# Cross attention of a perceiver: text probabilities and value sums turned together with the image probabilities, one DMA back, queries made per batch

## What is computed

```python
def attend(q, k, v):                       # scale 64 ** -0.5
    attn = softmax(einsum('bihd,bjhd->bhij', q, k) * SCALE)
    return einsum('bhij,bjhd->bihd', attn, v)
out = attend(x @ Wq, txt @ Wk, txt @ Wv) + attend(x @ Wq, img @ Wk_ip, img @ Wv_ip)
x = x + out @ Wo + bo                      # text and image have a softmax each
```

## Time and profile before

| | |
|---|---|
| median of 3 runs | 2453.11 us (2441.91 to 2453.33) |
| the profiled execution | 2435.73 us |
| its span (first to last instruction) | 2433.6 us |
| PE busy, share of the span | 2160.2 us, 89% |
| DVE busy | 1570.4 us, 65% |
| ACT busy | 925.0 us, 38% |
| POOL busy | 877.5 us, 36% |
| mean granted TensorE clock | 0.94 of full speed |

### The profile page before, as it was taken

One profiled execution on the slowest core, in us unless ns is written; L12 is line 12 of the kernel. 1 busy time (PEld: TensorE's weight loads), 2 busy tenths in 40 slices (PEclk: granted clock), 3 DMA queues, 4 the chain that ended last, 5 costly groups with the idle time before them and its releaser, 6 DMA issues. The chain is left out here.

```text
span 2433.6 us, 37422 instructions
## 1 busy us (share of the span) xinstructions
PE 2160.2 (89%) x13637; PEld 1726.1 (71%) x13637; DVE 1570.4 (65%) x2756; ACT 925.0 (38%) x1869; POOL 877.5 (36%) x535
## 2 busy tenths in 40 slices
PE   5878877796699999999999999999999997787897
PEld 3445545464598889888898998998998994334684
DVE  4179934333577677677677677777776763795554
ACT  1166611210244344344344444444443443452331
POOL 1066412431343333243343333343333300362455
PEclk8989977798899999999999999999999998798898
DMA  5800002511476677677676777776776656001364
GB/s 159 169 16 14 8 1 88 230 50 57 145 200 184 185 218 205 185 217 206 185 217 180 226 202 208 198 207 199 202 211 186 194 156 248 4 0 44 98 148 114
DMA packets 229957, 362.99 MB, mean 149 GB/s; under 512 B 41920, under 2 KB 197824, under 8 KB 225168
## 3 DMA queue, kind: packets, MB, share of 16 engines
q1 hardware_dynamic: 223008, 342.08, 48.1%
q0 software_dynamic: 6768, 18.49, 3.2%
HBM read 234.97 MB, written 125.50 MB: 148 GB/s over the span
## 5 line engine op out<-in xcount | busy, mean ns | idle before, releaser
L2271 PE MATMUL img_ps<-cn,pt_hi 128*128 128x256 f32 (+1 forms) x3072 | 569.7, 287 | 3.0 <-DVE pt_lo L2478 3.0
L2271 PEld LDWEIGHTS img_ps<-cn,pt_hi 128*128 128x128 f32 (+1 forms) x3072 | 477.3, 191 | 3.2 <-issue 3.2
L2271 PE MATMUL img_ps<-cn,pt_lo 128*128 128x256 f32 (+1 forms) x1536 | 435.9, 284 | 0.0
L2466 DVE STREAM_TRANSPOSE prob_blocks<-prob 128x384 f32<-128x384 f32 x512 | 250.6, 547 | 183.8 <-ACT prob L2402 175.9
L2248 PE MATMUL s_ps<-ct,a_hi 128*128 128x508 f32 x768 | 315.7, 411 | 0.0
L2249 PE MATMUL s_ps<-ct,a_hi 128*128 128x508 f32 x768 | 304.2, 396 | 0.0
L2250 PE MATMUL s_ps<-ct,a_lo 128*128 128x508 f32 x768 | 304.0, 396 | 0.0
L2001 POOL TENSOR_SCALAR ct<-staged 128x762 fp32r<-128x762 f32 x64 | 136.8, 2138 | 439.6 <-DMA staged<-in_ctx_t 312.5
L2271 PEld LDWEIGHTS img_ps<-cn,pt_lo 128*128 128x128 f32 (+1 forms) x1536 | 292.6, 190 | 0.0
L2478 DVE TENSOR_TENSOR pt_lo<-prob_moved,pt_hi 128x768 fp32r<-128x768 f32 x256 | 277.9, 1124 | 9.4 <-ACT pt_hi L2414 9.2
L2001 POOL TENSOR_SCALAR cn<-staged 128x768 fp32r<-128x768 f32 x64 | 137.4, 2147 | 376.5 <-DMA staged<-in_ctx_n 293.4
(11 more groups left out here) (370 smaller groups left out, 3712.9 us busy)
## 6 DMA issues: line engine op xcount, KB each, us to landing
prob_rows<-prob_blocks SPq DMA_DIRECT2D x512, 192.0 KB, 2.1
prob_moved<-prob_rows SPq DMA_DIRECT2D x512, 192.0 KB, 3.6
staged<-in_ctx_n SPq DMA_DIRECT2D x64, 384.0 KB, 4.7
staged<-in_ctx_t SPq DMA_DIRECT2D x64, 381.0 KB, 4.7
up_all_m<-in_up SPq DMA_DIRECT2D x8, 2048.0 KB, 12.8
down_all_m<-in_down SPq DMA_DIRECT2D x8, 1024.0 KB, 23.4
sums_m<-y_b SPq DMA_DIRECT2D x63, 128.0 KB, 2.2
w_shared<-in_wq SPq DMA_DIRECT2D x7, 1024.0 KB, 7.3
```

Source lines behind the costliest of these rows:

```text
L2271: last = nc.tensor.matmul(img_ps[:, 0:D], left[0:n, j, :], rows[0:n, right, j, :], start=j == 0 and at == 0, stop=j == IB - 1 and at == 2)
L2466: nc.vector.transpose(blocks[:, m], source[:, m]).then_inc(turned, 1)
```

## The change

- **One bundle.** `prob` grows from 12 to 15 blocks of 128 columns: 12 of image probabilities, one of text probabilities, two of the sums. The four DVE transposes, the stores and the return carry all of them. Text (of step `g-2`) and sums (of step `g-2`) are put into `prob` by ACT and DVE in turn `g` and leave with bundle `g+1`. So `turn_text`, `turn_sums`, their PSUM banks and the copies `pt_txt` and `ot` go, and `value_side` runs one turn later and reads `moved` itself.
- **Stores and return.** Each of the four parts is stored as 32 rows of each of four row groups (`block_rows[s, m]`, read as `c a f`), so that the whole bundle comes back with one DMA, 7680 bytes to a partition. `moved` is one buffer, not two: the return of bundle `g` waits until `pt_lo` of step `g-1` is made (`split_done`), until `value_side(g-4)` is copied out (`valued`), and until all four parts are stored.
- **Sums.** `img_ps` is used over its full width: one matmul of 512 columns takes `pt_hi` with the high and the low part of `cn`, and one of 256 columns adds `pt_lo` with the high part into the second half. ACT scales the second half into `o_part`, DVE scales the first and adds `o_part` (SCALAR_TENSOR_TENSOR), into `prob`.
- **Text.** The exponentials of the text go to three buffers `txt_prob`; ACT, no longer DVE, multiplies them by the reciprocal.
- **Queries per batch.** `queries(b)` makes one batch (64 columns) in one bank, at the end of the 7th and the 14th turn of a tile, and ACT alone copies it. `wq` and `wo` are loaded in halves, `wq` after the returns of the 5th and 6th turn, `wo` after those of the 15th and 16th.
- `project` comes two turns later than before and stands behind `key_side`.

```diff
+    TXT_AT, O_AT = IB, IB + 1
+    BUNDLE = IB + 1 + C
+    RUN = BUNDLE * QR
+    LAG = 3
-        block_rows = nc.dram_tensor("prob_rows", (2, Q, P, RUN), F32).ap()
-        moved = [sb(f"prob_moved{s}", [P, Q, IB, QR]) for s in range(2)]
+        block_rows = nc.dram_tensor("prob_rows", (2, Q, QR, Q, RUN), F32).ap()
+        moved = sb("prob_moved", [P, Q, BUNDLE, QR])
...
+            return {6: 2 * i + 1, 13: 2 * i + 2 if i < NT - 1 else None}.get(n) if g < N else None
...
-            for g in range(N):
+            for g in range(N + LAG):
                 if g >= 2:
-                    sp.wait_ge(moved_in[s], 16 * Q * (g // 2))
+                    sp.wait_ge(moved_in, 16 * (g - 1))
                 for m in range(Q):
                     sp.wait_ge(turned, Q * g + m + 1)
-                    sp.dma_start(block_rows[s, m], blocks[:, m].rearrange("p j r -> p (j r)")).then_inc(stored[m], 16)
-                if g >= 2:
-                    sp.wait_ge(split_done, 2 * (g - 1))
+                    sp.dma_start(block_rows[s, m].rearrange("c a f -> a c f"),
+                                 blocks[:, m].rearrange("p j r -> p (j r)")).then_inc(stored[m], 16)
+                if g:
+                    sp.wait_ge(split_done, 2 * min(g, N))
+                if g > LAG:
+                    sp.wait_ge(valued, g - LAG)
                 for m in range(Q):
                     sp.wait_ge(stored[m], 16 * (g + 1))
-                    sp.dma_start(moved[s][m * QR:(m + 1) * QR].rearrange("c a j r -> c a (j r)"),
-                                 block_rows[s, m].rearrange("(a c) f -> c a f", a=Q)).then_inc(moved_in[s], 16)
+                sp.dma_start(moved[:].rearrange("p a j r -> p (a j r)"),
+                             block_rows[s].rearrange("m c a f -> (m c) (a f)")).then_inc(moved_in, 16)
...
-                        for at, (left, right) in enumerate(((pt_hi, 0), (pt_hi, 1), (pt_lo, 0))):
-                            last = nc.tensor.matmul(img_ps[:, 0:D], left[0:n, j, :], rows[0:n, right, j, :],
-                                                    start=j == 0 and at == 0, stop=j == IB - 1 and at == 2)
+                        nc.tensor.matmul(img_ps[:], pt_hi[0:n, j, :], rows[0:n, :, j, :], start=j == 0, stop=False)
+                        last = nc.tensor.matmul(img_ps[:, D:2 * D], pt_lo[0:n, j, :], rows[0:n, 0, j, :],
+                                                start=False, stop=j == IB - 1)
...
+                pe.wait_ge(moved_in, 16 * (g + LAG + 1))
...
-                        nc.tensor.matmul(out, wv[:, c, cols], ot[:, c, rows], start=c == 0, stop=False)
+                        nc.tensor.matmul(out, wv[:, c, cols], moved[:, rows, O_AT + c, :], start=c == 0, stop=False)
...
+                    nc.scalar.activation(o_part[:], img_ps[:, D:2 * D], ACT.Copy,
+                                         scale=inv[(g - 2) % 3][:, 1:2]).then_inc(part_kept, 1)
+                    act.wait_ge(turned, Q * min(g + 1, N + LAG))
+                    nc.scalar.activation(prob[:, TXT_AT * P:TXT_AT * P + TXT], txt_prob[(g - 2) % 3][:], ACT.Copy,
+                                         scale=inv[(g - 2) % 3][:, 0:1]).then_inc(txt_normed, 1)
...
+                    nc.vector.scalar_tensor_tensor(out=prob[:, O_AT * P:], in0=img_ps[:, 0:D],
+                                                   scalar=inv[(g - 2) % 3][:, 1:2], in1=o_part[:], op0=ALU.mult,
+                                                   op1=ALU.add).then_inc(sums_kept, 1)
```

More of the change, by code:

```diff
@@ L2209, in kept, with queries @@
                 pe.wait_ge(t_kept[place[0]], place[1])
[L2211 to L2221, removed]
+            def queries(b):
+                bank = use()
+                for p in range(PAIRS1):
+                    for c in range(C):
+                        last = nc.tensor.matmul(t_ps[bank][:, p * S:(p + 1) * S], wq[:, c, p * P:(p + 1) * P],
+                                                k.h_t[:, c, b * S:(b + 1) * S], start=c == 0, stop=c == C - 1)
+                last.then_inc(t_done[bank], 1)
+                return ring.place(1)
             def key_side(g):
@@ L2311, in _ @@
             pe.wait_ge(wq_in, 16)
[L2312 removed]
+            q_place = queries(0)
             pe.wait_ge(wk_in, 16)
[L2314 to L2315 removed]
+            kept(q_place)
             a_place = key_side(0)
[L2317 removed]
+            for g in range(N + LAG + 2):
                 if g < N:
@@ L2386, in keep_a, with keep_queries @@
                 nc.scalar.activation(flat(a_hi), t_ps[bank][:, 0:D], ACT.Copy).then_inc(a_hi_kept, 1)
+            def keep_queries(b):
+                bank, count = ring.next()
+                act.wait_ge(t_done[bank], count)
+                act.sem_inc(queried, 1)
+                for r in range(2):
+                    rows = slice(r * HD1, (r + 1) * HD1)
+                    last = copy(q[rows, :, b % 2, r, :], t_ps[bank][rows, :].rearrange("p (j n) -> p j n", j=PAIRS1))
+                last.then_inc(t_kept[bank], 1)
             act.wait_ge(q_zeroed, 1)
-            keep_queries(act, copy, 0, ring)
+            keep_queries(0)
             keep_a(0)
-            for g in range(N + 3):
-                if 1 <= g <= N:
-                    keep(act, copy, ring, pt_txt[(g - 1) % 3][0:TXT, :], TXT, P)
-                if g >= 3:
-                    keep(act, copy, ring, flat(ot), P, D)
-                if not boundary(g) and g < N - 1:
+            for g in range(N + LAG + 2):
+                if g < N - 1:
                     keep_a(g + 1)
+                if projects(g) is not None:
+                    ring.next()
+                    ring.next()
                 if g < N:
@@ L2440, in _ @@
             nc.vector.memset(q[:], 0.0).then_inc(q_zeroed, 1)
-            dve.wait_ge(q_zeroed, 1)
-            keep_queries(dve, copy, 1, ring)
-            dve.sem_inc(queried, 1)
+            ring.next()
             keep_a_lo(0)
             dve.wait_ge(pad_zeroed, 1)
-            for g in range(N + 3):
+            for g in range(N + LAG + 2):
                 if g < N:
```

198 lines of the change are left out of this document (81 added, 117 removed).

## The result

The changed kernel takes 3348.37 us (median of 4 runs, 3343.68 to 3354.96); the kernel before, beside it on the same chip, 2452.89 (4 runs, 2441.91 to 2453.33). The ratio is 1.3667, 95% interval 1.3622 to 1.3712: slower by more than a third, far outside the forecast range (2398 to 2474). The profiled execution has a span of 3352.9 us.

A forecast was written before the change was run, and what follows sets the result against it. PE was taken to set the pace, at 10.1 us a plain step. Terms of -56 + 12 - 41 - 6 - 5 + 53 + 10 + 8 gave -25 us from 2453, so 2428 us, range 2398 to 2474.

The forecast's parts named there:

- Why not all of it: DVE's longer transposes and the single `moved` in each step: return issued at 13.2 us, occasional stalls, +12 us.
- The return is late: Rival: the single return takes 7.0 us, steps average 10.4 us, +80 us, 2508 us; chance 0.10.
- The store itself: Fourth store of a step, issued at 10.9 us, lands 2.1 to 2.4 us later.
- A plain step: Step without tile end: transposes go, sums get cheaper, 0.45 us less, 9.66 us; -56 us over 124 steps.
- The 0.1 us for contention and late returns: Added to a mean step for POOL disturbing DVE and returns landing late: +12 us.
- Queries: Batches of 64 columns at 0.11 us a matmul, 3.55 us a batch, fifteen inside the steps: +53 us.
- The half-price rival: Query matmuls of 64 columns cost half, 1.8 us a batch; with `wq` in time 2392 us; chance 0.11.
- `wq` in halves: Second half of `wq` lands late for the 7th turn's queries: 1.5 us in each of seven tiles, +10 us.
- Project: `project` no longer waits for the copy of `head_out`: 0.6 us each for eight, -5 us.
- The end: After the last step three more bundles in series, each return before the next: +8 us (4 to 14).
- POOL in every step: Rival: POOL between the halves of `pt_lo` each step, +42 us, 2470 us, chance 0.15; by the skill's rule 2631, 0.02.
- my sum of 25 us less: All terms together: -25 us, 2411 us for an execution like the profiled one, 2428 us for the timed runs.

The follow-up runs named there:

- whole_stores_one_return: Changed kernel with each part taking every fourth element of a block, stored as 128 rows in partition order, single return kept: 2570.67 us, ratio 1.0494.
- four_returns: Changed kernel with each part stored as one run of 128 whole rows and four returns, as in the kernel before: 2537.66 us, ratio 1.0392.
- two_moved_wq_at_once: four_returns with both halves of `wq` issued in one turn and two `prob_moved` in turn, `wv` half as wide: 2458.54 us, ratio 1.0035.
- long_queries: four_returns with 128 moving columns for each query matmul where 64 are wanted: 2553.22 us (one run).
- the two of early queries: Kernel before with a tile's queries a step earlier, projection a step later: ratio 0.9892; the same plus sums as 512 and 256 columns: 0.9863.

## Why the prediction was wrong

The step that failed is in "Why not all of it": "the fourth store is issued at 10.9 and lands 2.1 to 2.4 later, so the return is issued at 13.2". I took the landing of a store of 192 KB from rows of before and scaled nothing but its size. But the same edit turned its pattern from 128 rows in one dimension into `4x32x480`, a row that stood in my own view of SP's order. In the changed kernel the return is issued some 11 us after the fourth store. The Trainium skill, DMA: Bandwidth & Descriptors, "Why a DMA increments its semaphore by 16 and not by 1", says that the engines of such a DMA are the largest number up to 16 that divides the slowest dimension on both sides, and the lowest-numbered ones; its "Rules for kernel authors" warn of just this. The traces agree in number: 4 of 16 at `4x32`, 2 at `2x32`, and both halves on the same two; which of the sixteen they are, no trace here tells. I had it as no rival. The nearest, "The return is late", was worked out for a return of 7.0 us, and the return took the 4.9 that I had forecast. What it said of the consequence came true, PE waiting ahead of `value_side`, but from a cause that it didn't have: counted from the fourth store the return has landed after 11 + 4.9 = 15.9 us, where my sum had 2.3 + 4.9 = 7.2 and this rival 2.3 + 7.0 = 9.3.

The other terms, on kernels whose stores use all engines:

- *The store itself*, 2.1 to 2.4 forecast: 2.3 us in whole_stores_one_return, 2.8 in four_returns.
- *A plain step*, 9.66 forecast: the undisturbed ones take 9.75, 0.09 more; block of the sums 0.35 as forecast.
- *The 0.1 us for contention and late returns* was far too small: the mean was to be 9.76, and ordinary steps of four_returns (second to eighth tile) have 10.51 us, with two buffers 10.07, of which 16.3 us / 46 steps = 0.35 are late returns still. It is the second mis-sized term; the condition was named, the frequency (a return late in 32 of 43 steps, 0.7 us each, in 1000 to 1500 us of four_returns) was not.
- *Queries*: 3.79 us a batch at full clock, 3.55 forecast, the same for 64 columns as for 128 (long_queries, 14th turn). The half-price rival is wrong.
- *`wq` in halves*: 1.59 us measured (10.3 in all seven tiles), 1.5 forecast. What I missed was the clock behind it: 2.6 us in the queries, and some 2 in the next step.
- *Project*: 13.26 - 9.75 = 3.5 us over a plain step, 14.41 - 10.10 = 4.3 before: 0.8 saved each, 0.6 forecast.
- *The end*, +8 forecast: from the last step's start to the end of the last addition 32.9 us before, 88 in the changed kernel (below), and with all engines at the stores still 51 (two_moved_wq_at_once, returns at 2020.14, 2027.51 and 2035.24, 7.5 us apart). Each bundle there is a store, a landing, a return and a landing in series; I had counted the returns alone.
- *POOL in every step*: not seen; `pt_lo` has a median of 0.96 us for a half in four_returns and 0.95 in whole_stores_one_return, as in a quiet step.

```profile
2850.65 0.45 PE L2245 MATMUL s_ps<-k_txt,q 128*128 128x77 f32 x2
...
2938.62 0.29 DVE L2462 TENSOR_TENSOR x_sb<-x_sb,t_ps 128x128 f32<-128x128 f32 x1 [2.03 <-PE t_ps L2301]
```

Of the 896 us, some 775 to 810 are the store's pattern (two repairs of it, with one return or four). The rest, about 90 us, is the single buffer (84, with its clock), against which the forecast gains are set. After both repairs the time is that of before (ratio 1.0035) and so some 33 us above my sum of 25 us less. An estimate of where they are, from the steps: 83 ordinary ones of 10.07 where I had 9.76 are 26 us, and the end, longer by 18 where I had 8, is 10.

I can't say how the 414 us that the changed kernel spends behind the last addition come to be 14 more than before. It doesn't go with the change: the same code took 400 to 402 us in five of the thirteen profiled executions and 411 to 415 in eight, the two of early queries among these.

## What to carry to other kernels

When an edit reshapes a DMA, price it by its new access pattern and not by the size of the old one: read the outermost dimension in the order of the issuing queue, and the busy share and the rate in a stretch where only that transfer runs. A share of 0.26 over all of the stretch was here a pattern that uses four engines, not a queue that is full. And look for the part of a change that stands by itself: here it was the earlier queries, 1.1% without any of the rest.

## What I had not expected of the hardware

- Four engines gave 99 GB/s and two 49, about 25 each. With a share of 1.0 and more the windows of four_returns above show 398 GB/s in one stretch and 232 in another, so a share of 1.0 alone doesn't tell the rate.
- Behind 1.5 to 2 us of idle time on PE the granted clock went from 1.00 to 0.50, and the 32 query records behind took 6.38 us for 3.79. The 1.59 us of waiting cost some 4.6 us more behind them. Not each such wait did it: in the kernel before, PE stood idle for 1.88 us ahead of the text score at 1326.46, and the clock was still 1.00 from 1326 to 1329 us.
- A stride of 16 bytes in the source of a DVE transpose of 32-bit values costs 60%: 3.79 us for 2.36.
